# A graph kernel's scale statistics in the prologue, all pieces of x by squares, and scaled weights stored in two halves

## The reference, cut to what matters

```
# layer 0, applied twice with (W0, b0) and (W1, b1): mean over incoming edges, then a dense layer
neigh = segment_sum(vals[:, None] * x[cols], rows)          # vals = 1 / degree
x = relu(concatenate([x, neigh], axis=1) @ W.T + b)
# then x = layernorm(x + layer0(x))
h_self, h_neigh = feat @ W_self, feat @ W_neigh
h_sparse = h_neigh with all but the 32 largest of each row set to 0
neigh = segment_sum(h_sparse[src], dst) / maximum(deg, 1)
# out = layernorm(x + h_self + neigh)
```

## Time and profile before

| | |
|---|---|
| median of 3 runs | 675.32 us |
| the profiled execution, its own time | 673.44 us |
| its span in the profile | 671.6 us |
| what lies around the span | 1.8 us |
| mean granted TensorE clock | 0.993 |
| prologue, to the first `fill(1, 0)` | 0 to 33.2 us |
| building of C | 33.2 to about 180 us |
| layers | about 180 to 671.6 us |

### The profile page before, as it was taken

One profiled execution on the slowest core, in us unless ns is written; L12 is line 12 of the kernel. 1 busy time (PEld: TensorE's weight loads), 2 busy tenths in 40 slices (PEclk: granted clock), 3 DMA queues, 4 the chain that ended last, 5 costly groups with the idle time before them and its releaser, 6 DMA issues.

```text
span 671.6 us, 10824 instructions
## 1 busy us (share of the span) xinstructions
PE 635.9 (95%) x3782; PEld 323.6 (48%) x3783; DVE 498.8 (74%) x1274; ACT 314.5 (47%) x604; POOL 110.0 (16%) x187
## 2 busy tenths in 40 slices
PE   8788899999978999999999899999999999999996
PEld 3466566666533444444444344444444444444442
DVE  7888979999778888888863678787887846633333
ACT  3678799999667766666641222222222210000000
POOL 3001122222111110101000232323223110000000
PEclk9989999999999999999999999999999999999999
DMA  8543644555612222322223999999999933300000
GB/s 215 101 141 110 218 138 159 166 181 162 186 56 58 60 56 56 60 53 65 50 60 95 165 208 174 206 177 186 192 173 187 178 90 116 116 25 26 27 25 23
DMA packets 66741, 79.61 MB, mean 119 GB/s; under 512 B 30320, under 2 KB 59407, under 8 KB 66681
## 3 DMA queue, kind: packets, MB, share of 16 engines
q1 hardware_dynamic: 66681, 78.86, 54.9%
HBM read 38.91 MB, written 33.38 MB: 108 GB/s over the span
## 4 chain that ended last, share of the span: by engine, by line
PE 66%; DVE 15%; DMA 9%; ACT 4%; issue 3%; POOL 2%; SPq 1%; DVEq 0%; POOLq 0%; ACTq 0%
PE pair L1550 23%; PE bank L1648 10%; PE pair L1648 10%; PE bank L1474 6%; DMA tr_sb<-part 5%; PE bank L1445 4%; PE pair L1365 4%; PE bank L1453 3%; PE pair L1453 3%; DMA own_in<-own_dram 2%; DVE m L953 2%; DVE hots L648 2%; DVE work L958 2%; POOL part L556 1%; DVE tree L831 1%
## 5 line engine op out<-in xcount | busy, mean ns | idle before, releaser
L1550 PE MATMUL pair<-xs,ct 125*128 125x512 f16 x625 | 139.4, 379 | 2.3 <-issue 2.3
L1550 PE MATMUL pair<-a,ct 125*128 125x512 f16 x625 | 138.9, 379 | 0.0
L648 DVE TENSOR_TENSOR hots<-iota,jobs 125x1792 f16<-125x1792 f16 (+1 forms) x100 | 103.6, 1069 | 3.4 <-PE pair L1365 2.9
L1550 PEld LDWEIGHTS pair<-xs,ct 125*128 125x128 f16 x625 | 61.7, 99 | 75.0 <-issue 2.8
L1550 PEld LDWEIGHTS pair<-a,ct 125*128 125x128 f16 x625 | 62.0, 99 | 73.8
L1079 ACT ACTIVATE slab<-pair 125x875 f16<-125x875 f32 (+1 forms) x100 | 83.3, 854 | 11.3 <-PE pair L1365 6.8
L1231 ACT ACTIVATE a<-ct 125x1000 f16<-125x1000 f16 (+1 forms) x75 | 80.4, 1072 | 9.7 <-DMA c_dram<-slab 8.1
L538 POOL TENSOR_TENSOR own_in<-own_in,bias_sb 125x256 f32<-125x256 f32 x50 | 37.8, 757 | 246.5 <-DMA own_in<-own_dram 246.5
L1648 PE MATMUL bank<-xs,ct 125*128 125x512 f16 (+1 forms) x325 | 71.5, 379 | 0.0
L1648 PE MATMUL pair<-xs,ct 125*128 125x512 f16 x300 | 66.2, 379 | 0.0
L1299 ACT ACTIVATE sd<-mv,epsb 125x1 f32<-125x1 f32 x25 | 7.4, 294 | 113.9 <-DVE mv L1015 113.9
(11 more groups left out here) (202 smaller groups left out, 758.4 us busy)
## 6 DMA issues: line engine op xcount, KB each, us to landing
c_dram<-slab SPq DMA_DIRECT2D x25, 683.6 KB
ct<-c_dram SPq DMA_DIRECT2D x25, 683.6 KB
own_in<-own_dram SPq DMA_DIRECT2D x50, 125.0 KB
own_dram<-own SPq DMA_DIRECT2D x25, 125.0 KB
own_dram<-own_st SPq DMA_DIRECT2D x25, 125.0 KB
x_in<-in_x_dram SPq DMA_DIRECT2D x25, 125.0 KB
z_dram<-z_st SPq DMA_DIRECT2D x25, 125.0 KB
a<-z_dram SPq DMA_DIRECT2D x5, 625.0 KB
```

Of the source, the lines that this page charges most:

```text
L648: v.tensor_tensor(hots[k][:, :, :, :].rearrange("p w g (a d) -> p (w g) a d", d=2), iota, job, ALU.is_equal).then_inc(win_hot, 1)
L1550: ins = mm(agg[k % 3][0:lhs.shape[1], :], lhs, parts[l][:, t, :], start=t == 0, stop=t == NT - 1, skip_group_check=True)
```

## The change

SyncE loads pieces 2 and 3 of x behind wneigh, wself and b0. VectorE makes the fourth row sum (W1) and the maxima of wneigh after the one-hots of tile 0, and the maxima of b0 and wself after those of tile 1; `largest_x` is gone, and ScalarE squares all four pieces, each one place earlier, the first ahead of `jobs_out(0)`. `w_low` moves behind the next copy or one-hots. Each `w_parts` tensor is stored when its own two low parts are done (t = 4 and t = 5), and ScalarE waits for the stores ahead of `quick_copy(8, 3)`. The diff without the branch for edge lists that do not fit the fast path, which is not run here:

```diff
-            for c in range(4):
+            def load_x_piece(c):
                 for lo, hi in PARTS:
                     sp.dma_start(xs32[lo:hi, XC[c]:XC[c + 1], :], ...).then_inc(x_loaded[c], 16)
+            load_x_piece(0)
+            load_x_piece(1)
             sp.dma_start(wn_nat...)
             sp.dma_start(ws_nat...)
             sp.dma_start(bcol...)
+            load_x_piece(2)
+            load_x_piece(3)
...
                 store_slab(t)
-                if t == HELD - 2:
-                    sp.wait_ge(w_split, 4)
-                    for l in range(2):
-                        sp.dma_start(wparts_dram[l], w_parts[l]...).then_inc(w_stored, 16)
+                if 3 < t < 6:
+                    sp.wait_ge(w_split, 2 * t - 6)
+                    sp.dma_start(wparts_dram[t - 4], w_parts[t - 4]...).then_inc(w_stored, 16)
...
-            for l in range(2):
-                for h in range(2):
-                    at = 6 + 2 * l + h
-                    v.tensor_reduce(stat[:, at:at + 1], w_nat[:, l, h, :], X, ALU.add, ...).then_inc(w_sums, 1)
+            sum_w(0, 0)
+            sum_w(0, 1)
+            sum_w(1, 0)
             unpack(0)
...
             quick_hots(0, 3)
+            sum_w(1, 1)
+            largest_wn()
             unpack(1)
...
             quick_hots(1, 3)
+            largest_ws()
...
-                step(v.tensor_scalar(sv[:, 0, 0:3].bitcast(I32), sv[:, 0, 0:3].bitcast(I32), ...
+                step(v.tensor_scalar(sv[:, 0, 0:4].bitcast(I32), sv[:, 0, 0:4].bitcast(I32), ...
...
                         quick_hots(t + 1, 0)
-                    if t == 1:
-                        largest_x(3)
...
                     tr_copy(t - 1, 1)
-                    if 3 < t < 6:
-                        w_low(2 * t - 8)
                     if more:
                         quick_hots(t + 1, 1)
-                    if t == 1:
-                        largest_w()
                     if t == 3:
                         scales_out()
                     if 3 < t < 6:
-                        w_low(2 * t - 7)
+                        w_low(2 * t - 8)
...
                     tr_copy(t - 1, 3)
+                    if 3 < t < 6:
+                        w_low(2 * t - 7)
...
             slots_out(0)
+            act.wait_ge(const_ready, 10)
+            square_x(0)
             jobs_out(0)
-            act.wait_ge(const_ready, 11)
-            square_x(0)
+            square_x(1)
             slots_out(1)
             quick_copy(0, 0)
             quick_copy(0, 1)
-            square_x(1)
+            square_x(2)
...
                 quick_copy(0, FILLS - 1)
-                square_x(2)
+                square_x(3)
                 for t in range(1, NT):
-                    if t == HELD:
-                        act.wait_ge(w_stored, 32)
...
+                    if t == HELD:
+                        act.wait_ge(w_stored, 32)
                     quick_copy(t, 3)
...
             def bounds_t():
-                pe.wait_ge(squared, 3)
-                pe.wait_ge(stat_ready, 4)
+                pe.wait_ge(squared, 4)
+                pe.wait_ge(stat_ready, 3)
```

More of the change, by code:

```diff
@@ L358, in _ @@
                 store_slab(t)
-                if t == HELD - 2:
-                    sp.wait_ge(w_split, 4)
-                    for l in range(2):
-                        sp.dma_start(wparts_dram[l], w_parts[l][:, :, :, :].rearrange("p h q f -> p (h q f)")
-                                     ).then_inc(w_stored, 16)
+                if 3 < t < 6:
+                    sp.wait_ge(w_split, 2 * t - 6)
+                    sp.dma_start(wparts_dram[t - 4], w_parts[t - 4][:, :, :, :].rearrange("p h q f -> p (h q f)")
+                                 ).then_inc(w_stored, 16)
             for o in OWN[NT - 1]:
@@ L656, in _, with sum_w, largest_wn, largest_ws @@
             dve.wait_ge(const_ready, 10)
-            for l in range(2):
-                for h in range(2):
-                    at = 6 + 2 * l + h
-                    v.tensor_reduce(stat[:, at:at + 1], w_nat[:, l, h, :], X, ALU.add, apply_absolute_value=True).then_inc(w_sums, 1)
+            def sum_w(l, h):
+                at = 6 + 2 * l + h
+                v.tensor_reduce(stat[:, at:at + 1], w_nat[:, l, h, :], X, ALU.add, apply_absolute_value=True).then_inc(w_sums, 1)
+            def largest_wn():
+                dve.wait_ge(wn_loaded, 16)
+                v.tensor_reduce(stat[:, 12:14], wn_nat[:, :, :], X, ALU.max, apply_absolute_value=True
+                                ).then_inc(stat_ready, 1)
+            def largest_ws():
+                dve.wait_ge(b_loaded, 16)
+                v.tensor_reduce(stat[:, 14:16], bcol[:, :].rearrange("p (h o) -> p h o", o=1), X, ALU.max,
+                                apply_absolute_value=True).then_inc(stat_ready, 1)
+                dve.wait_ge(eye_added, 2)
+                v.tensor_reduce(stat[:, 10:12], ws_nat[:, :, :], X, ALU.max, apply_absolute_value=True
+                                ).then_inc(stat_ready, 1)
+            sum_w(0, 0)
+            sum_w(0, 1)
+            sum_w(1, 0)
             unpack(0)
@@ L731, in general_table @@
                 v.tensor_copy(table[:, :, :], rows[:, 0:2, :]).then_inc(table_ready, 1)
-            def largest_x(c):
-                dve.wait_ge(x_loaded[c], BOTH)
-                v.tensor_reduce(stat[0:P, c:c + 1], xs32[:, XC[c]:XC[c + 1], :].rearrange("p t f -> p (t f)"), X, ALU.max,
-                                apply_absolute_value=True).then_inc(stat_ready, 1)
-            def largest_w():
-                dve.wait_ge(b_loaded, 16)
-                v.tensor_reduce(stat[:, 14:16], bcol[:, :].rearrange("p (h o) -> p h o", o=1), X, ALU.max,
-                                apply_absolute_value=True).then_inc(stat_ready, 1)
-                dve.wait_ge(wn_loaded, 16)
-                v.tensor_reduce(stat[:, 12:14], wn_nat[:, :, :], X, ALU.max, apply_absolute_value=True
-                                ).then_inc(stat_ready, 1)
-                dve.wait_ge(eye_added, 2)
-                v.tensor_reduce(stat[:, 10:12], ws_nat[:, :, :], X, ALU.max, apply_absolute_value=True
-                                ).then_inc(stat_ready, 1)
             def bound_rows():
@@ L764, in bounds @@
                 step(v.tensor_copy(sv[:, :, :], bank[6][0:1, 0:2 * NST].rearrange("p (a b) -> p a b", a=2)))
-                step(v.tensor_scalar(sv[:, 0, 0:3].bitcast(I32), sv[:, 0, 0:3].bitcast(I32), 0.5, float((127 << 22) + (16 << 23)),
+                step(v.tensor_scalar(sv[:, 0, 0:4].bitcast(I32), sv[:, 0, 0:4].bitcast(I32), 0.5, float((127 << 22) + (16 << 23)),
                                      ALU.mult, ALU.add))
```

## The result

The changed kernel took 671.3 us (median of 5 runs, 668.88 to 672.17), the kernel before 675.42 us (median of 5, 674.93 to 677.74). The ratio is 0.9922, with an interval of 0.9901 to 0.9943: 5.3 us less by the ratio, between 3.8 and 6.7 (the two medians differ by 4.1). The forecast was 670.6 us, from 668.6 to 673.8. The changed kernel was run again beside the first experiments: 669.05 us, ratio 0.9928 (0.9901 to 0.9954). The profiled execution of the first took 672.17 us (span 670.4) and that of the second 668.85 us (span 667.0), where the one of before took 673.44 us (span 671.6).

A forecast was written before the change was run, and what follows sets the result against it. TensorE was taken to bound the layers, behind 180 us, so gains lay in its waits before. Terms 0.7 - 1.2 - 1.5 - 2.7 = -4.7 us took 675.3 to 670.6 us, range 668.6 to 673.8.

The forecast's parts named there:

- Tile 8: ScalarE's wait for the two w_parts stores goes, since halves are issued earlier and ScalarE asks three copies later: -2.7 us.
- Tile 1: Removing the three largest_w reductions saves 1.2 us (0.6 to 1.25); removing the maximum over piece 3 saves 0.
- Tiles 4 to 6: Low parts no longer directly behind their high parts remove idle time of VectorE and ScalarE: -1.5 us (0.5 to 1.75).
- Prologue: Earlier wself load moves GpSimd's two additions beside the one-hots of tile 0: +0.7 us (0 to 1.3).
- The meeting of the additions with the one-hots: In tile 0, GpSimd's additions slow VectorE beside them; two meetings would cost 1.0 us, 0.7 taken.
- nothing to spare: Before unpack(1), moved VectorE work of 1.22 to 1.30 us just fills the 1.30 us idle; later delay costs fully.
- The end: After 83 us waits are relative and TensorE is full, so the whole -4.7 us reaches the end.
- No meeting: Prologue rival: wself lands beside single-input work, additions are free; -5.6 us, giving 669.7 us; chance 0.12.
- The halves stand in front of the slabs: Rival: halves issued right ahead of slabs make ScalarE wait in two of tiles 6 to 8; +2.5 us, 677.8; chance 0.05.
- the things named as making the forecast wrong: ScalarE waiting for c_dram stores in tiles 6 to 8, late x pieces or largest_wn load, or a second half-clock stretch.

The follow-up runs named there:

- wait_only: Kernel before with only ScalarE's wait for both stores moved from its first to its last slab copy of t = 8; 672.27 us, ratio 0.9969.
- stats_only: Changed kernel with low parts and stores as before, leaving the load order, squares and moved reductions; 674.3 us, ratio 0.9987 against the kernel before.
- wlow_only: Kernel before with only the four low parts moved behind the next copy or one-hots; 672.76 us, ratio 0.9969.
- stats_stores: Changed kernel with only the low parts put back in their old places; 671.8 us, ratio 0.9934 against the kernel before.
- again: The changed kernel, unaltered, run for a second profile and more times; 669.05 us, ratio 0.9928 against the kernel before.
- pad_branch: Changed kernel with 24 semaphore increments on ScalarE in a branch never taken, moving the code behind it; 668.11 us, ratio 0.9906 against the kernel before.
- warm_both: Changed kernel with five more unused matmuls in the prologue and ten in the gap ahead of tile 1; 669.04 us, ratio 0.9898 against the kernel before.
- act_shift: Changed kernel with 24 executed increments of an unused semaphore on ScalarE at the start of the layers; 671.85 us, ratio 0.9938 against the kernel before.

## Why the prediction was right, and where not

**The total** was forecast as 4.7 us less; the ratios say 5.3 and 4.9, the medians 4.1 and 6.0, the two profiled spans 1.2 and 4.6. Its largest terms held. That it came so near is in part luck, since its errors nearly cancelled.

**Tile 8** (-2.7, measured -2.68) was right in size, and read from the right pair of rows: the same work in tiles 8 and 12. The step names two causes, the halves being issued earlier and ScalarE asking three copies later, and did not ask whether both are needed. wait_only shows that the second alone does all of it; by the landing times the first alone would have, too, which no run tests.

**Tile 1** (-1.2, measured -1.06 over tiles 1 to 3, and -1.24 in stats_only): right in size. The maximum over piece 3 was costed at nothing and the late maxima at 1.2. Tile 1 itself was not shorter, as the forecast had it: it grew by 0.46, at half clock, and tile 2 went from 6.33 to 4.90. That fits the late maxima, which stood from 39.19 to 40.44 us, around the start of tile 2 (40.07), but no run separates the two.

**Tiles 4 to 6** (-1.5, measured -1.11 with tile 7, shown twice: by wlow_only and by stats_stores). The mis-sized term. The wait itself went as reckoned: VectorE's idle time in tiles 4 to 7 fell from 24.41 - 22.49 = 1.92 us to 23.30 - 22.90 = 0.40, so by 1.52. But its busy time rose by 0.41, and that is one operation: the first low part, moved behind the one-hots, met an addition of GpSimd and took 1.16 us for 0.76 (the other three took 0.73 or 0.74, before 0.75). The step looked at the wait that the move took away, and not at what stands on GpSimd at the new place.

**Prologue** (+0.7, measured -0.35): the step that failed, in its sign. The meeting of the additions with the one-hots was foretold, its place too, and its price of 0.7 was not far off: VectorE lost 0.44. What failed is that this price was put on the path, with a wait for `row` that had "nothing to spare". The wait had room for it: it was 0.22 us longer than reckoned, since the one-hots began that much earlier against TensorE's `fill(0, 0)`, where the forecast had them at the same place, and the two reductions took 1.19 us. So the 0.44 cost nothing. And what the additions had cost beside `unpack(1)` was overlooked: two operations of 0.56 us that take 0.42 alone. That is the 0.28 that came back, of 0.35.

The rule of the Trainium skill ("SBUF — State Buffer", shared port pair), weighed there as up to 1.3 us, has the one that starts second wait for the other's whole instruction. The trace agrees, instruction by instruction (again): one-hots from 18.58 to 19.67 us, not stretched; the addition that began beside them at 18.85 ended at 19.98; the next one-hots, from 19.59 to 20.80, took 1.21 for 1.09; and the addition that began at 19.95 ended at 21.11. So each side waits in turn, and the whole loss of one side is not the length of the other's work: the additions took 1.39 us longer, VectorE 0.44.

**The end.** "After 83 us all waits are relative and TensorE is full, so it reaches the end" failed by 1.05 us: TensorE's first pass over C takes 1.4 us longer (174.5 against 173.1), what lies around it 0.35 less. It is ScalarE's second stop at the start of the layers, which pad_branch takes away. The errors sum to nearly nothing: 1.05 us to the good in the prologue and 0.45 by an early `fill(0, 0)`, against 0.14 in tiles 1 to 3, 0.39 in tiles 4 to 7, 0.02 in tile 8 and 1.05 behind tile 9.

**The rivals.** "No meeting" came nearest in the prologue (0 for the measured -0.35), and for the wrong reason. "The halves stand in front of the slabs" didn't come: SyncE's rows in the changed kernel (again) are

```profile
61.19 0.35 SPq L366 DMA_DIRECT2D wparts_dram<-w_parts  x1
...
65.40 0.74 SPq L354 DMA_DIRECT2D c_dram<-slab  x2
...
67.67 0.35 SPq L366 DMA_DIRECT2D wparts_dram<-w_parts  x1
...
70.45 0.74 SPq L354 DMA_DIRECT2D c_dram<-slab  x2
```

so each half had 4.2 and 2.8 us before the next slab, and ScalarE waited for no store. Of the things named as making the forecast wrong one came in the first profile, a second stretch at half clock; wlow_only has it too, with the prologue of before.

## What to carry to other kernels

Before a transfer is split or moved to come earlier, try to move the wait for it to the first instruction that needs it: here one line gave what two edits were meant to give. When an operation of VectorE is moved, look at what GpSimd does at the new place and at the old one, and whether what is lost there falls into a wait: the two terms that were most off were such meetings. And after any edit look once at the far end of the program, behind the branches: here an unchanged stretch lost a microsecond because code had moved.

## What the runs showed of the hardware

- **The clock goes with much of the spread.** Of the kernel before, executions with a mean granted clock of 0.993 or 0.994 took 672.55 to 675.01 us, and those at 0.984 to 0.986 took 677.42 to 679.55. Of the changed kernel four executions at 0.994 took 668.85 to 669.19, one at 0.992 took 668.12, and those at 0.987 to 0.991 took 670.44 to 672.87. It is not all of it: the six executions of warm_both, at 0.995 to 1.000, took 667.35 to 671.59, the longest of them at 0.997. In the 14 profiles the low stretches (0.50, the 1.2 of 2.4 GHz) lie in the prologue (3), in tile 1 (11), in tile 3 (7), in tile 8 (1) and in the layers, near 196 us (1), between 368 and 377 us (7) and at the very end (1, pad_branch). The one in tile 1 is in every profile but the three with ten added matmuls in the idle time ahead of it; the one in the prologue is in one of the two profiles of the changed kernel and not in the other.
- **VectorE and GpSimd.** Beside additions of GpSimd two one-hots took 0.26 us more, and the two additions 2.26 us for 0.87; a low part took 0.40 more and the addition beside it 0.62 more than the 0.67 of the earlier trace rows; f32 operations in the prologue took 0.14 more each. In the first meeting of the earlier trace rows the addition started first (88.67 us, VectorE 88.70): it took its 0.67 and VectorE lost the 0.5. Where one-hots were under way first, they kept their time, the addition ended late and the operation behind the one-hots lost.
- **Where code lies.** 24 instructions that are never executed changed the time of a stage by 1.3 us. Behind a taken branch ScalarE stood still for 6.7 to 7.9 us in all 14 profiles, even in front of increments that wait for nothing (act_shift), and went on 1.27 to 1.41 us after an 8 KB transfer on the instruction queue.
